# Fourier layers of a token network: narrower column-tiled forward transforms, another layout of the squares, and new instruction orders in a pair

## The reference, cut to what matters

```python
h = layer_norm(x @ fc0_w + fc0_b, ln0_g, ln0_b)          # 3 -> 32 channels
for i in range(4):
    x_ft = rfft2(h)                                      # only 24 x 12 modes are kept
    x1 = irfft2(einsum('bixy,ioxy->boxy', x_ft, w[i]))   # mix of channels per mode
    x2 = einsum('bchw,oc->bohw', h, conv_w[i]) + conv_b[i]
    h = layer_norm(x1 + x2, ln_g[i], ln_b[i])            # over the 32 channels
    if i < 3:
        h = gelu(h)
h = gelu(h @ fc1_w + fc1_b); h = gelu(h @ fc2_w + fc2_b); h = h @ fc3_w + fc3_b
```

## Time and profile before

| | |
|---|---|
| median of 3 runs | 3,216.27 us (3,214.8 to 3,220.66) |
| the profiled execution, its own time | 3,222.97 us |
| its span, from the first to the last instruction | 3,221.1 us |
| PE busy | 2,893.1 us (90%) |
| DVE busy | 2,215.7 us (69%) |
| ACT busy | 2,148.5 us (67%) |
| POOL busy | 2,102.1 us (65%) |
| granted PE clock, mean | 0.965 |

### The profile page before, as it was taken

One profiled execution on the slowest core, in us unless ns is written; L12 is line 12 of the kernel. 1 busy time (PEld: TensorE's weight loads), 2 busy tenths in 40 slices (PEclk: granted clock), 3 DMA queues, 4 the chain that ended last, 5 costly groups with the idle time before them and its releaser, 6 DMA issues. The chain is left out here.

```text
span 3221.1 us, 190782 instructions
## 1 busy us (share of the span) xinstructions
PE 2893.1 (90%) x80542; PEld 1961.7 (61%) x80542; DVE 2215.7 (69%) x3767; ACT 2148.5 (67%) x3644; POOL 2102.1 (65%) x1147
## 2 busy tenths in 40 slices
PE   6777999997999999699999689999999987999997
PEld 4555777775677777477777534444444424666665
DVE  7765889884888887488898444444444436777775
ACT  4663777774677776477777257777777764666654
POOL 3763899993899997499999344445445434666664
PEclk9997999998899999899999889999999998999998
DMA  5764555554455554455555411111211103111111
GB/s 164 229 224 142 172 173 176 181 172 142 148 176 179 171 181 143 146 175 174 177 175 179 137 52 53 58 55 58 58 55 58 58 21 79 31 30 30 30 30 24
DMA packets 236925, 379.78 MB, mean 118 GB/s; under 512 B 117090, under 2 KB 154786, under 8 KB 236530
## 3 DMA queue, kind: packets, MB, share of 16 engines
q1 hardware_dynamic: 225122, 363.94, 36.7%
q10 hardware_dynamic: 7920, 10.03, 1.0%
q0 software_dynamic: 3744, 3.84, 0.8%
HBM read 217.88 MB, written 159.83 MB: 117 GB/s over the span
## 5 line engine op out<-in xcount | busy, mean ns | idle before, releaser
L1481 POOL TENSOR_TENSOR rstd<-var,mhalf 128x16 f32<-128x16 f32 x512 | 1524.3, 2993 | 694.3 <-DVE var L1238 688.8
L1238 DVE TENSOR_REDUCE var<-sq 128x16 f32<-128x528 f32 x384 | 403.3, 1051 | 93.0 <-ACT sq L903 93.0
L1252 DVE TENSOR_TENSOR zt<-ps,rstd 128x512 f32<-128x512 f32 x512 | 345.1, 684 | 77.8 <-POOL rstd L1481 71.4
L615 PEld LDWEIGHTS ps<-d,hp 128*32 128x32 f32 x24576 | 292.0, 111 | 132.2 <-ACT hp L915 97.3
L615 PE MATMUL ps<-d,hp 128*32 128x48 f32 x24576 | 345.0, 209 | 27.2 <-ACT hp L915 15.2
L544 PEld LDWEIGHTS ps<-cwl,hc 64*64 64x64 f32 x16384 | 272.3, 139 | 139.6 <-issue 133.5
L527 PE MATMUL ps<-zb,ex 48*128 48x512 f32 x1024 | 305.0, 672 | 51.2 <-DVE zt L1252 20.5
L555 PEld LDWEIGHTS ps<-dyi,gt 64*48 64x48 f32 x16384 | 230.1, 124 | 164.2 <-issue 152.5
L1074 ACT ACTIVATE a<-ps,fc1b 128x1024 f32<-128x1024 f32 x256 | 271.1, 1110 | 64.8 <-PE ps L818 64.8
L544 PE MATMUL ps<-cwl,hc 64*64 64x64 f32 x16384 | 308.2, 226 | 0.0
L903 ACT ACTIVATE sq<-ps 128x512 f32<-128x512 f32 x384 | 218.9, 598 | 132.9 <-PE ps L544 123.8
(11 more groups left out here) (199 smaller groups left out, 4800.6 us busy)
## 6 DMA issues: line engine op xcount, KB each, us to landing
h_scratch<-ho SPq DMA_DIRECT2D x256, 512.0 KB
hc<-h_scratch SPq DMA_DIRECT2D x256, 512.0 KB, 4.2
wsb<-in_w SPq DMA_DIRECT2D x64, 288.0 KB
gin<-g_scratch SPq DMA_DIRECT2D x252, 72.0 KB
gin<-g_scratch SPq DMA_DIRECT2D x504, 36.0 KB
wc<-expert_scratch SPq DMA_DIRECT2D x64, 129.0 KB, 2.7
g_scratch<-hp ACTq DMA_DIRECT2D x32, 192.0 KB, 4.5
g_scratch<-hp SPq DMA_DIRECT2D x32, 192.0 KB, 4.1
```

The lines of the kernel that those rows point to most:

```text
L615: last = nc.tensor.matmul(a_ps[row:row + 32, 2 * TRIG * k:2 * TRIG * k + 2 * TRIG], hp[b][:, u, 8 * j + k].rearrange("p v r -> p (v r)"), ...
L1238: nc.vector.tensor_reduce(dst, src, axis=AX.X, op=ALU.add).then_inc(var_ready, 1)
L1252: nc.vector.tensor_tensor(by_px(zt[h][:, u]), by_px(main_ps(s, h, u)), scale, ALU.mult).then_inc(norm_ready, 1)
L1481: nc.gpsimd.tensor_tensor(rstd[u][:], var[u][:], mhalf[:], ALU.pow).then_inc(rstd_ready, 1)
```

## The change

Constants `dx` (real and imaginary half of the x transform, 24 columns each) and `dy` (two halves of 24 columns) are loaded beside `d1` and `cy`, which the stem still uses.

- f1: two batches of 16 channels instead of four of 8. Each 32-column tile of PE gets one part (real or imaginary) of one unit, with 24 moving columns. There are as many matmuls as before. `a_copy` is done twice a pair, 384 contiguous columns each.
- `asb` is one buffer, channel by frequency. f2 loads 32 channels of one frequency (a step of 24 values) and streams `dy[:, part]` into four column tiles: twice as many matmuls, half as wide. The rows of `xsb`, and with them the weights, `sgn` and the stem's constants, are ordered by part, then channel.
- `sq[u]` has the channel innermost: square reads PSUM with a step of 16 values and writes contiguous rows; reduce reads contiguous rows.
- New orders on PE, ACT, DVE and POOL, as in the diff.
- The rows that `mix` writes get a tile of their own (`grow`) in place of `asb[1]`. One more small centring step runs at the start.

```diff
-        asb = [sb(f"asb{p}", [128, 2 * KX, C, 2]) for p in range(2)]
-        sq = [sb(f"sq{u}", [128, C + 1, 16]) for u in range(2)]
+        asb = sb("asb", [128, C, 2 * KX])
+        grow = sb("grow", [128, 2 * 768])
+        sq = [sb(f"sq{u}", [128, 16, C + 1]) for u in range(2)]
...
-                 (ident, t["ident"]), (d1, t["d1"]), (cy, t["cy"])]
+                 (ident, t["ident"]), (d1, t["d1"]), (cy, t["cy"]), (dx, t["dx"]), (dy, t["dy"])]
...
-                pe.wait_ge(a_ready, 4 * rank(s, g) + j)
-                for k in range(8):
-                    for a in range(2):
+                pe.wait_ge(a_ready, 2 * rank(s, g) + j)
+                for k in range(CH):
+                    for part in range(2):
                         for u in range(2):
-                            row = 64 * a + 32 * u
-                            last = nc.tensor.matmul(a_ps[row:row + 32, 2 * TRIG * k:2 * TRIG * k + 2 * TRIG],
-                                                    hp[b][:, u, 8 * j + k].rearrange("p v r -> p (v r)"),
-                                                    d1[:, a].rearrange("p x s -> p (x s)"),
+                            row = 64 * part + 32 * u
+                            last = nc.tensor.matmul(a_ps[row:row + 32, 2 * KX * k:2 * KX * k + 2 * KX],
+                                                    hp[b][:, u, CH * j + k].rearrange("p v r -> p (v r)"), dx[:, part],
                                                     start=True, stop=True, tile_position=(0, row))
...
                 for a in range(6):
                     for c in range(2):
-                        o = KY * (6 * m + a)
-                        last = nc.tensor.matmul(x_ps[64 * c:64 * c + 64, o:o + KY],
-                                                asb[b][:, KX * m + 2 * a + c].rearrange("y c s -> y (c s)"),
-                                                cy[:], start=True, stop=True, tile_position=(0, 64 * c))
+                        for part in range(2):
+                            o, row = KY * (6 * m + a), 64 * c + 32 * part
+                            last = nc.tensor.matmul(x_ps[row:row + 32, o:o + KY], asb[:, :, KX * m + 2 * a + c],
+                                                    dy[:, part], start=True, stop=True, tile_position=(0, row))
...
                     if here:
                         widen(s, 0, g, 1)
+                        conv(s, 0, g, 1)
+                        with where_next(g):
+                            i1(s, g + 1, 0, CH)
                     if old:
                         f1(s, 0, g - 1, 0)
-                    if here:
-                        conv(s, 0, g, 1)
-                    for j, piece in enumerate(((0, 6), (6, 11), (11, 16))):
-                        if here:
-                            with where_next(g):
-                                i1(s, g + 1, *piece)
-                        if drain:
-                            keep_awake(z_mid[0], 128, 2)
-                        if old and j == 2:
-                            turn(s, 0, g - 1, 1, 0)
-                        if old:
-                            f1(s, 0, g - 1, j + 1)
+                    if drain:
+                        keep_awake(z_mid[0], 128, 3)
+                    if old:
+                        turn(s, 0, g - 1, 1, 0)
+                        f1(s, 0, g - 1, 1)
...
-                    dst = sq[u][:, 0:C, :].rearrange("p (v c) n -> p v (c n)", v=2)
+                    dst = sq[u][:, :, 0:C]
+                by_px = (lambda tile: tile.rearrange("p (v n) -> p v n", v=2)) if is_last(s) else (
+                    lambda tile: tile.rearrange("p (c n) -> p n c", c=C))
+                nc.scalar.activation(dst, by_px(main_ps(s, h, u)), ACT.Square).then_inc(sq_ready, 1)
...
-                    dst, src = var[u][:], sq[u][:].rearrange("p c n -> p n c")
+                    dst, src = var[u][:], sq[u][:]
```

## The result

The changed kernel took 3,182.5 us (median of four runs, 3,179.1 to 3,187.1) against 3,217.7 for the kernel before in the same session: a ratio of 0.989, 95% interval 0.987 to 0.991. It is faster, as forecast, but by 35 us and not by 76. All medians and ratios are of fast runs, those that show no slower second state of the chip. The profiled run took 3,181.5 with a span of 3,179.7, 41.4 less than the 3,221.1 of before; this is the difference that the traces have to explain.

What follows compares the result with a forecast made beforehand. PE was taken as the closer bound (13.9 us a pair), POOL within 4%. Passes -71, pass ends -7, start +2: -76 on 3,223.0 gives 3,147, less 6.7 is 3,140 us; 3,110 to 3,170 without more surprises, full range 3,085 to 3,205.

Steps and rivals of the forecast that it cites:

- the rival of the strided read: ACT's square reading PSUM with a 64-byte step costs 1.25 us; period 14.0 to 14.3, 3,175 to 3,205 us; chance 0.14.
- f1's batch at 1.30: PE's f1 as two batches of 128 instructions with 24 columns, 1.30 us each: 3.28 a pair becomes 2.60.
- the three loops: PE 13.25, POOL 13.3 and the ring 13.0 us a pair, almost equal and tied to each other at several places.
- PE's own sum: PE's steps in one pair added up after the change: 13.25 us, or 12.95 to 13.7 with f1's bounds.
- The period of 13.65: Time per image pair in the passes: 13.3 plus 0.35 for ties, down 0.76 from 14.41 us.
- ties: Time a pair lost where the loops hold each other up: 0.5 us before, taken as 0.35 after.
- the ring: Loop of gin loads, ACT's coefficients to hc_copy, then store and load_h on SP's queue: 12.95 us, between 11.6 and 13.9.
- Landing: Time for the gin loads to arrive after issue, in the ring: taken as 3.3 us, between 1.9 and 4.2.
- the forecast's own rival: The gin ring is longer, with landing 4.2: 13.9 us plus ties, period 14.1, 3,185 us; chance 0.08.
- Two rounds of f1, copy, f1 go: -2.5 x 3: At each pass's end, two of four uncovered rounds, each some 1.5 us, disappear: -7 us over three passes.
- w_centre costs nothing: POOL's w_centre moved between two rstds: its weights and w_sum should be ready in time, so no added cost.
- the strided rival: f2's weights strided by 96 bytes slow PE: old period at 1.42 us a half; 3,420 us at 53 ns; chance 0.07.

Runs made afterwards that it cites:

- e2: The changed kernel with SP's order alone changed: one store each half step, issued behind the loads; 3,158.0 us, 0.981 of the kernel before.
- e9: e2 with the centring for the last couple of a pass moved behind its last rstd; 3,161.2 us, 0.982 of the kernel before.
- e11: e10 with f2's weights contiguous and ACT's copy writing with a step of 128 bytes instead; 3,151.5 us, 0.980 of the kernel before.
- e1: The changed kernel with POOL's centring of the mixing weights back in its old place; 3,217.7 us, 1.000 of the kernel before.
- e3: The changed kernel with POOL's power over 8 of 16 columns in all passes but the last; 3,237.1 us, 1.005 of the kernel before.
- e14: e2 with the layers' gains and biases left out, as one-input operations on DVE in the passes; 3,126.9 us, 0.970 of the kernel before.
- e10: e9 with the sign product of the mixing weights moved from POOL to ACT in the passes; 3,139.1 us, 0.975 of the kernel before.

## Why the prediction was right and wrong

**Right.** The reduce (0.70 forecast, 698 ns measured) and the square (0.62, 600 ns, so the rival of the strided read is out). f1's batch at 1.30, measured 1.21 to 1.28. The direction and the range. POOL as the longest of the three loops once nothing disturbs it. PE's own sum was 13.25 in the forecast and is 12.9 (i1 took 1.57 and not 1.75, f1 1.21).

**Right by luck.** The period of 13.65, which e2 shows at 13.67. The forecast had 13.3 of POOL's work and 0.35 for ties. In e2 POOL's own work is 13.65, and it waits 0.5 us in 300 for a variance: the work was taken too low and the ties too high by the same amount.

**Wrong, first: the ring.** The step that failed is the sum "12.95, between 11.6 and 13.9". Measured it is 13.81 by its own legs, in the pair shown: issue and landing 6.55 against 6.0, ACT 5.52 against 5.0, hc_copy to gin 1.74 against 1.75. Landing was taken at 3.3 between two bounds, and it was 3.8 (412.74 less the last issue's end at 408.92), near to the upper one. ACT's leg had no wait for a conv in it. With these the ring is the longest loop, not the shortest, and the forecast's own rival gives 14.1 a pair and 3,185 us. The result was 13.93 and 3,182.5, and e2, which takes the ring away, is 25 us faster. I had given that rival 0.08; with a middle of the ring 0.35 below POOL and an upper bound 0.6 above it, it deserved more.

**Wrong, second: the drain.** "Two rounds of f1, copy, f1 go: -2.5 x 3" became +4.1 x 3. The rounds did go. What the step didn't ask is what else the change had put into the drain: two batches of 128 matmuls with their loads, behind which PE stands still for 2.9 us a drain; a centring between two of the last rstds, which holds a gelu, ACT in its order behind it and PE for 2.7 us; and a clock that falls after that wait. Moving that centring away gave back only 1.0 (e9), since the last gelus then came late. "w_centre costs nothing" was true of the loop with its cover, and the drain has no cover.

**Wrong in size.** f2's weights: the stride was held to be free by comparison with the turn's loads. e11 shows that it costs 0.35 us a half, but 0.90 from start to start is only 0.06 above the 0.84 that the copies ask anyway, so the sum hardly noticed. The reason against the strided rival was wrong; its point of decision, 1.42 a half, was not reached. POOL: 13.65 and not 13.3, by its meetings with gains and biases. The earlier trace rows were read as a middle pass with POOL at 83%, but they go on into the drain and the mix; inside the pass it was at 90% already.

**What stays open.** Why e1 and e3 lengthen ACT's leg of the ring was seen (waits for PE) but not traced to a first cause. Whether a second input has any part in what a gain does to POOL. That the code's loading causes the stalls rests on their place, their shift by four and the packets; no run took the loading away.

## What to carry to other kernels

Write down every ring that goes through an in-order queue, with the load's landing at its upper bound, before you call it slack; one blocked store ahead of the loads was worth 25 us here, and a reordering of two lines on another engine had brought it on. Cost an edit at the edge of a loop as well as in its middle: where the cover ends, a moved instruction, a lower clock and code that is not yet loaded each show. When two loops are within 3% of each other, test a bound only after the other one is removed: the shorter power did not shorten the couples in one order and made the kernel 45 us faster in the other. And read the granted clock before a slower run is put down to a wait: of the 55 us by which e3 was slower, some 49 were PE at 1.2 GHz behind waits of 1 to 2 us. The best version, e13, is the changed kernel with SP's stores behind the loads, the sign on ACT, the last centring late and two more fillers a drain, and takes 3,133 us, 0.972 of the kernel before.

## What the hardware showed that was not expected

- A GpSimd instruction that begins while VectorE does an elementwise operation from SBUF to SBUF with two inputs (gain, bias) is longer by what is left of that operation, less 0.14 us: 0.56 in place of 0.28 us, 0.88 in place of 0.67, or 3.1 to 3.4 in place of 2.9. Beside the one-input forms of e14 powers still take 3.01 to 3.12. Beside a reduce, a normalise or a copy out of PSUM nothing is added.
- Waits of PE of 1.1 to 2.2 us inside a pass were followed by 3 to 7 us at a granted clock of 0.50 (e3), and a couple with such a stretch took 2.35 us more on average.
- ScalarE reads PSUM with a step of 64 bytes at no cost (512 elements in 600 ns, 598 contiguous), but writing SBUF with a step of 128 bytes takes 819 in place of 479 ns for 384 elements (e11).
- Four column tiles of 32 load strided weights at 162 ns a load on the trace and contiguous ones at 111; a batch of 48 takes 0.97 and 0.62 us.
- TensorE in straight-line code stood still up to 2.4 us at a block of 16 KB of instructions (e10), and went on 1.3 to 1.5 us after the block's DMA packet ended.
- The power on GpSimd takes 2.9 us for 128x16 and 1.64 to 2.01 for 128x8.
